# Four tables of cycle numbers and two residual adds in the tail of an S4D and mixture-of-experts block

## The reference

```python
out = jnp.zeros_like(x)
for e in range(E):
    ew = jnp.sum(topk_weights * (selected_experts == e), axis=-1, keepdims=True)
    h = x @ w1[e].T
    gate = jax.nn.silu(h[:, :I])
    y = h[:, I:] * gate @ w2[e].T
    out = out + y * ew
...
x = x + _layernorm(out)      # the mean and the variance of each token's 128 channels
```

## Time and profile before

| | us |
|---|---|
| median of 3 runs | 1006.62 |
| lowest and highest | 1004.01, 1007.06 |
| the profiled execution's own time | 1013.19 |
| its span, first to last instruction | 1011.1 |
| busy in the span: PE, DVE, ACT, POOL | 762.7, 698.1, 487.8, 464.5 |

### The profile page before, as it was taken

How to read it: one execution, slowest core, us unless ns; L and a number is a source line. 1 busy time by engine, 2 the same in 40 slices (tenths; PEclk the granted TensorE clock), 3 DMA queues, 4 the chain that set the end, 5 groups by cost and what they waited for, 6 DMA issues and landing times.

```text
span 1011.1 us, 23854 instructions
## 1 busy us (share of the span) xinstructions
PE 762.7 (75%) x8401; PEld 665.1 (66%) x8402; DVE 698.1 (69%) x1778; ACT 487.8 (48%) x1009; POOL 464.5 (46%) x672
## 2 busy tenths in 40 slices
PE   0029618799486994869857798676999999999991
PEld 0018518667386764857557576565899999999881
DVE  8996876759668596667966589875453335555677
ACT  7726971039610595105930169763234444563355
POOL 2102314426543365424643358665655553456560
PEclk9999859979798897979979799656999999999995
DMA  7804699992599916999089910011134444443122
GB/s 276 314 0 114 189 374 385 350 376 104 185 388 334 390 59 239 387 339 385 3 296 386 410 53 2 24 48 55 64 116 143 143 145 139 137 119 121 46 74 102
DMA packets 115519, 197.47 MB, mean 195 GB/s; under 512 B 17500, under 2 KB 38504, under 8 KB 114792
## 3 DMA queue, kind: packets, MB, share of 16 engines
q1 hardware_dynamic: 108776, 182.62, 51.1%
q0 software_dynamic: 6656, 13.64, 4.6%
HBM read 164.38 MB, written 31.85 MB: 194 GB/s over the span
## 4 chain that ended last, share of the span: by engine, by line
PE 36%; issue 25%; POOL 18%; DVE 12%; ACT 5%; DMA 2%; POOLq 1%; another core or an unknown queue 1%; SPq 0%; ACTq 0%; DVEq 0%
PE bank L1246 15%; PE bank L1263 9%; POOL zbuf L661 7%; POOL rstd_of L650 5%; PE bank L1095 3%; PE bank L1073 2%; PE bank L1218 2%; POOL sums L641 1%; DMA toep<-kernels_dram 1%; PE bank L1165 1%; POOL mean_of L646 1%; POOL m L648 1%; ACT ln_tmp L939 1%; ACT toep L950 1%; PE bank L1153 1%
## 5 line engine op out<-in xcount | busy, mean ns | idle before, releaser
L1095 PE MATMUL bank<-zbuf,toep 128*128 128x128 f16 (+3 forms) x3328 | 141.9, 204 | 94.8 <-DVE zbuf L1473 72.2
L1095 PEld LDWEIGHTS bank<-zbuf,toep 128*128 128x128 f16 x3328 | 138.7, 101 | 98.6 <-issue 48.2
L1246 PE MATMUL bank<-toep 128*128 128x256 f16 x1452 | 170.4, 274 | 7.5 <-DVE toep L1749 5.2
L1830 DVE TENSOR_TENSOR glu_work<-bank,glu_work 128x512 f32<-128x512 f32 x121 | 80.1, 688 | 136.5 <-ACT glu_work L987 94.2
L1246 PEld LDWEIGHTS bank<-toep 128*128 (+1 forms) x1452 | 141.6, 98 | 26.1 <-issue 5.2
L661 POOL TENSOR_TENSOR zbuf<-zbuf,w_cur 128x256 f32<-128x256 f32 x120 | 90.1, 752 | 141.5 <-DVE zbuf L1537 141.4
L987 ACT ACTIVATE glu_work<-bank 128x512 f32<-128x512 f32 x121 | 68.5, 596 | 162.3 <-PE bank L1246 142.0
L1130 PE MATMUL bank<-wo_cur,glu_work 128*128 128x256 f32 x512 | 134.8, 408 | 2.5 <-ACT glu_work L884 2.2
L1537 DVE TENSOR_REDUCE zbuf<-bank 128x256 f32<-128x512 f32 x128 | 87.0, 687 | 69.9 <-PE bank L1095 69.9
L721 POOL DMA_INDIRECT z_sorted<-toep x104 | 102.1, 982 | 65.6 <-PE bank L1246 32.1
L1130 PEld LDWEIGHTS bank<-wo_cur,glu_work 128*128 128x128 f32 x512 | 96.3, 198 | 44.3 <-issue 17.3
(11 more groups left out here) (266 smaller groups left out, 1369.8 us busy)
## 6 DMA issues: line engine op xcount, KB each, us to landing
toep<-kernels_dram SPq DMA_DIRECT2D x104, 1024.0 KB, 14.0
glu_work<-kernels_dram SPq DMA_DIRECT2D x16, 1024.0 KB, 14.1
toep<-z_sorted SPq DMA_DIRECT2D x73, 128.0 KB
y_sorted<-toep SPq DMA_DIRECT2D x73, 128.0 KB
toep_last<-kernels_dram SPq DMA_DIRECT2D x8, 1024.0 KB, 14.1
z_sorted<-ln_tmp SPq DMA_DIRECT2D x2, 3584.0 KB, 26.8
hres<-in_x SPq DMA_DIRECT2D x1, 4096.0 KB, 12.8
toep<-in_x SPq DMA_DIRECT2D x1, 4096.0 KB, 22.2
```

Of the source, the lines that this page charges most:

```text
L1095: last = MM(dst[:, d * (B // 4):, :], toep_slot(g)[:, c, d * P:(d + 1) * P, k], z_conv[:, 0:QUADS - d * (B // 4), g * GROUP + c].rearrange ...
L1246: last = MM(out[:, piece % 2 * XP:(piece % 2 + 1) * XP], w1_row[:, pw, weights_at(s, piece * P, P)], xT_s[:, px * XP:(px + 1) * XP], start ...
L1830: TT(inner[:, s.at % 4, :], bank[3 + s.at % 2 * 2][:, :], gate_act[:, s.at % 2, :], ALU.mult).then_inc(s_inner, 1)
```

## The change

The tables are rewritten from cycle 112 on, the last three groups of moments become four, and two of the 16 residual adds go to GpSimd.

```diff
-SUM_AT = {0: 58, 3: 60, 1: 64, 2: 68, 4: 80, 5: 86, 6: 90, 7: 96, 8: 102, 9: 108, 10: 114, 11: 118, 14: 122, 12: 124, 15: 126,
+SUM_AT = {0: 58, 3: 60, 1: 64, 2: 68, 4: 80, 5: 86, 6: 90, 7: 96, 8: 102, 9: 108, 14: 112, 10: 114, 11: 120, 12: 126, 15: 126,
           13: 128}
-NORM_GROUPS = ((0, 16), (16, 20), (36, 12), (56, 8), (48, 8))
-MOMENTS_AT = (70, 104, 120, 126, 128)
-ROOT_AT = (72, 106, 122, 128, 130)
-SHIFT_AT = (74, 108, 124, 130, 132)
-NORM_AT = {0: 76, 1: 78, 2: 80, 3: 82, 4: 110, 5: 112, 6: 114, 7: 116, 8: 118, 9: 126, 10: 128, 11: 130, 14: 132, 15: 132,
-           12: 134, 13: 134}
+NORM_GROUPS = ((0, 16), (16, 20), (36, 8), (44, 8), (56, 8), (52, 4))
+MOMENTS_AT = (70, 104, 116, 126, 126, 128)
+ROOT_AT = (72, 106, 118, 128, 128, 130)
+SHIFT_AT = (74, 108, 120, 130, 130, 132)
+NORM_AT = {0: 76, 1: 78, 2: 80, 3: 82, 4: 110, 5: 112, 6: 114, 7: 116, 8: 118, 9: 122, 10: 124, 11: 132, 12: 132, 14: 132,
+           15: 132, 13: 134}
+BY_POOL = (11, 14)
...
+            for q in BY_POOL:
+                tiles = slice(4 * q, 4 * q + 4)
+                pool.wait_ge(s_last, 4 * (NORM_ORDER.index(q) + 1))
+                nc.gpsimd.tensor_tensor(hres[:, tiles, :], y_of(0, 4 * q, 4), hres[:, tiles, :], ALU.add).then_inc(s_res_pool, 1)
...
-                    if s.turn is None and NORM_AT[q] + 2 == s.at:
+                    if s.turn is None and NORM_AT[q] + 2 == s.at and q not in BY_POOL:
```

More of the change, by code:

```diff
@@ L466, in build @@
         s_h_in, s_h = sem("first_norm_in"), sem("h_ready")
-        s_res, s_out = sem("result_ready"), sem("out_stored")
+        s_res, s_res_pool, s_out = sem("result_ready"), sem("result_ready_by_pool"), sem("out_stored")
         glu16 = glu_work.rearrange("p a b n -> p (a b n)").bitcast(F16).rearrange("p (s g l k) -> p s g l k", s=2, g=GROUP, k=2)
@@ L595, in _ @@
                         store(tile)
-            for i, q in enumerate(NORM_ORDER):
+            by_dve = [q for q in NORM_ORDER if q not in BY_POOL]
+            for q in NORM_ORDER:
                 tiles = slice(4 * q, 4 * q + 4)
-                sp.wait_ge(s_res, i + 1)
+                if q in BY_POOL:
+                    sp.wait_ge(s_res_pool, BY_POOL.index(q) + 1)
+                else:
+                    sp.wait_ge(s_res, by_dve.index(q) + 1)
                 sp.dma_start(out[:, tiles, :], hres[:, tiles, :]).then_inc(s_out, 16)
```

## The result

The changed kernel takes 1013.16 us (median of 11 runs, 1008.03 to 1014.61), the kernel before 1006.08 in the same sessions (11 runs, 1000.64 to 1007.06). The ratio is 1.0075 with a 95% interval of 1.0057 to 1.0092: slower by 5.7 to 9.3 us. The forecast was slower too, by 4.05 us, and its range ended at 1012.8. The measured time lies outside it, and nearly half of the loss was not in my sum.

The account below looks back on a forecast made before the run. VectorE's queue up to the last variance was taken as the bound. 0.76 + 2.35 - 0.60 + 1.54 = +4.05 us took the span from 1011.1 to 1015.15 and the median from 1006.62 to 1010.7 us; range 1007.6 to 1012.8.

Parts of the forecast that it names:

- Step 1: Cycles 112 to 118: quad 14's statistics (0.78 us) and moments of quads 9 and 10 (0.81) are hidden, cost nothing.
- Step 2: Last silu, step 120: load, root and load (2.82 us) ahead of it start the last gated product 0.76 us later.
- Steps 3 to 5: Tail: VectorE's queue to the last variance +2.35 us, last variance to run -0.60, five quads normalised instead of four +1.54.
- Step 6: Two residual adds on GpSimd, about 1.5 us each: given zero; only over 3.7 us would quad 14's add cost anything.
- the loads cost nothing: Rival at the last silu: loads under way while ScalarE waits, +1.35 us in all, 1008.0; 5%.
- or more: Rival at the table loads: each switch also empties ScalarE's pipe, +2.6 us, 1013.3; 3%.
- a stall of before would be gone: Rival in cycles 102 to 106: one cycle's 6.18 us instead of 4.43 disappears, +2.3 us in all, 1008.9; 9%.
- The faster case: Rival in the tail: ScalarE's count of quads decides, five instead of seven, 3.1 us less, 1003.5; 4%.

Follow-up runs that it names:

- experiments 3: Kernel before with its own tables, residual adds of quads 9 and 10 moved to GpSimd: ratio 1.0031 (1.0007 to 1.0054), tail 27.37 us.
- experiment 6: Kernel before, all adds on VectorE, plus two GpSimd memsets of 512 elements to an unused tile: single execution, span 998.94 us, tail 25.96.
- experiment 1: Changed kernel with both residual adds back on VectorE: ratio 1.0057 (1.0033 to 1.0082), tail 29.98 us.

## Why the prediction was right and where it failed

*Direction: right.* The kernel is slower, and the three causes that the prediction priced (loads, VectorE's queue, the run of normalisations) are there at their sizes.

*Step 1, cover in cycles 112 to 118: held.* The product of step 114 was not late: VectorE even waits for ScalarE ahead of the product after it (0.62 us), and TensorE shows no wait there.

*Step 2, the loads: right in size.* The last silu came 2.83 us behind the normalisation (2.82 forecast). The price of 0.76 was taken from the end of a VectorE queue that was some 0.8 us late in that one trace. The normalisation ahead of the silu was late by as much, so the difference holds, and the undisturbed tail gives the same: the gated product begins 982.93 - 978.92 = 4.01 behind TensorE's product now, and 3.23 in experiments 3 and 6, 0.78 earlier. In the profile of before it was 4.00, which is why the two profiles differ by 7.1 and not 7.9. Moving that root alone back gave 1.85, more than 0.76, because the sum of quad 11 no longer stands where the gap is. The rule of the Trainium skill, "ScalarE: Activation LUTs", in its section on table sets, to batch calls by set, pointed the right way. The 1.38 us of draining that its section "What ACT_TABLE_LOAD costs" has for every switch were not paid here: load, root and load took 2.83.

*Steps 3 to 5, VectorE's queue, the roots in one piece, five quads in the run: right.* From the gated product to the last variance it is 14.47 us now and 12.18 in experiment 6: +2.29, and 2.35 forecast. From there to the run it is 0.51 in place of 1.11 (-0.60), and the run takes 7.80 in place of 6.27 (+1.53). All of it is tested together by experiment 1, the change without GpSimd: 29.98 - 25.96 = **4.02 us** over the undisturbed tail of before, where steps 1 to 5 add up to 4.05.

*Step 6, GpSimd: this is the step that failed.* I gave it zero and wrote that the add would have to take over 3.7 us to cost anything. The add was shorter than my estimate, 1.26 and not 1.5. But I asked only who waits for the add's data, and not what stands behind it in GpSimd's own list. Behind it was the DRAIN, 8.6 us long, of which 3.89 stuck out beyond the last store by experiment 1. The row was there to be read in the profile of before, at the line where the block ends: 11.1 us from 985.9, on an engine whose last work was over at 988.5. With it, my own estimate for the end of quad 14's add (1010.4) would have put the end of the DRAIN 8.5 us later at 1018.9, 3.8 us behind the 1015.15 of the sum. That makes 7.8 us, 1014.4 on the median used then, and the ratio's interval (5.7 to 9.3 us) holds it. "It can't be below zero" was true and the other bound was missing.

*The rivals.* That the loads cost nothing, or more, fell by the rows. That a stall of before would be gone did happen in the profiled execution, which was 5.5 us ahead by the first product of step 120. But the cycle of 6.18 us is gone in experiments 3 and 6 as well, which have the tables of before, and in the five traces with these tables that product begins anywhere from 972.98 to 984.37. So it comes and goes with the execution and is no effect of the change. The faster case fell as argued: VectorE had no slack to give, and ScalarE's run waited 3.24 us for it. None of the rivals had GpSimd's end in it.

## What to carry to other kernels

Work that is handed to an idle engine must be followed to the end of that engine's list, not only to the one who waits for its result: what the engine does when it is finished can be longer than the work. On GpSimd, after indirect transfers, end its list early and leave it alone. And when a step is moved ahead in a table, count what else is issued with it: a root in the wrong cycle brought two table loads in front of the one silu that the tail waited for, and a sum that had filled the gap was moved behind it.

Two executions can differ by more than the change. A fixed instruction close to the changed part, taken as the clock, gave differences good to some 0.1 us here, where ten runs gave 2.5 us. But look first whether the rows around that instruction agree between the traces: in the profile of before they did not, by 0.8 us.

## What the runs showed of the hardware that I had not expected

- GpSimd's last DRAIN lasts 0.07 us with no indirect transfer in the program, 0.74 with 8 gathers, 7.93 with 96, 8.42 with 208 and 9.16 with 104 gathers and 104 scatters, counted from the end of its last instruction, after the transfers have landed.
- GpSimd's add with two tiles read stopped VectorE's instructions with two SBUF inputs: 3.15 us in place of 1.13 for four of them, and 0.99 in place of 0.17 for a small one. A memset of GpSimd at the same place did not.
- After a wait of 2.80 us TensorE's granted clock was 0.50, and eight matmuls took 2.05 us in place of 1.13. After the same wait in another run they took 1.80.
